# Self-attention over 32 images on one core: another order of work for the first image

## The reference

```python
x = inputs.reshape(B, H * W, c)             # B=32, H*W=1024 tokens, c=256
q = x @ Wq + bq; k = x @ Wk + bk; v = x @ Wv + bv
scores = einsum('bnc,bmc->bnm', q, k) * c ** -0.5
out = (softmax(scores) @ v) @ Wo + bo
# what is returned, _gn being a group norm over 32 groups of 8 channels:
x + attention(_gn(x))
```

## Time and profile before

| | us |
|---|---|
| median of 3 runs (lowest, highest) | 1845.19 (1845.04, 1846.48) |
| the profiled execution | 1844.48 |
| its span, first to last instruction | 1842.8 |
| TensorE busy in the span | 1815.6 (99%) |
| VectorE busy | 1663.2 (90%) |
| ScalarE busy | 984.1 (53%) |
| mean granted clock of TensorE | 0.994 |

### The profile page before, as it was taken

The page is one execution under the profiler, slowest core; times in us unless marked ns, Lnnn a source line. Parts: engine busy times, 40 slices in busy tenths (PEclk is TensorE's granted clock), DMA queues, the critical chain, the costliest instruction groups (busy, mean ns, idle before and its releaser), DMA issues.

```text
span 1842.8 us, 32692 instructions
## 1 busy us (share of the span) xinstructions
PE 1815.6 (99%) x11562; PEld 1654.1 (90%) x11562; DVE 1663.2 (90%) x2921; ACT 984.1 (53%) x1347; POOL 92.1 (5%) x107
## 2 busy tenths in 40 slices
PE   8899999999999999999999999999999999999997
PEld 7799998999998998989999989989989999899896
DVE  5999999999999999999999999999999999999985
ACT  3645545646546556456455465465564554654652
POOL 0000000000000000000000000000000000000000
PEclk9999999999999999999999999999999999999998
DMA  3111222212222212222122222022221122220211
GB/s 114 58 51 29 68 57 68 68 26 54 68 57 68 62 18 68 57 68 68 36 44 68 57 68 67 12 68 62 63 68 43 37 68 57 68 68 17 62 24 24
DMA packets 29296, 101.92 MB, mean 55 GB/s; under 512 B 3681, under 2 KB 4706, under 8 KB 29282
## 3 DMA queue, kind: packets, MB, share of 16 engines
q0 software_dynamic: 9216, 33.56, 11.7%
q1 hardware_dynamic: 20066, 68.17, 11.2%
HBM read 68.16 MB, written 67.11 MB: 73 GB/s over the span
## 4 chain that ended last, share of the span: by engine, by line
PE 98%; DVE 1%; ACT 0%; DMA 0%; issue 0%; SPq 0%; POOLq 0%
PE ps_s L619 48%; PE ps_o L693 13%; PE ps_o L695 13%; PE ps_o L694 13%; PE ps_o L619 10%; DMA s_buf<-in_L_conv_bq_dram 0%; ACT p_hi L312 0%; ACT s_buf L318 0%; DVE s_buf L485 0%; DVE p_lo L493 0%; PE ps_o L631 0%; DVE s_buf L510 0%; DVE query_max L472 0%; SPq L217 0%; POOLq L66 0%
## 5 line engine op out<-in xcount | busy, mean ns | idle before, releaser
L693 PE MATMUL ps_o<-v_hi,p_hi 128*128 128x258 f32 x2048 | 580.6, 283 | 2.8 <-DVE p_lo L493 2.8
L695 PE MATMUL ps_o<-v_hi,p_lo 128*128 128x258 f32 x2048 | 581.1, 284 | 0.0
L694 PE MATMUL ps_o<-v_lo,p_hi 128*128 128x256 f32 x2048 | 578.4, 282 | 0.0
L312 ACT ACTIVATE p_hi<-s_buf 128x1024 fp32r<-128x1024 f32 x256 | 272.0, 1063 | 527.5 <-DVE s_buf L485 527.5
L619 PE MATMUL ps_s<-g_hi,h_hi 128*128 128x512 f32 x1024 | 399.7, 390 | 7.8 <-ACT s_buf L304 7.7
L619 PE MATMUL ps_s<-g_hi,h_lo 128*128 128x512 f32 x1024 | 400.4, 391 | 0.0
L619 PE MATMUL ps_s<-g_lo,h_hi 128*128 128x512 f32 x1024 | 399.8, 390 | 0.0
L693 PEld LDWEIGHTS ps_o<-v_hi,p_hi 128*128 128x128 f32 x2048 | 389.2, 190 | 5.7 <-issue 2.2
L694 PEld LDWEIGHTS ps_o<-v_lo,p_hi 128*128 128x128 f32 x2048 | 388.9, 190 | 3.0
L695 PEld LDWEIGHTS ps_o<-v_hi,p_lo 128*128 128x128 f32 x2048 | 388.7, 190 | 0.0
L304 ACT ACTIVATE s_buf<-ps_s 128x512 f32<-128x512 f32 x512 | 292.9, 606 | 170.2 <-PE ps_s L619 166.3
(11 more groups left out here) (84 smaller groups left out, 2199.5 us busy)
## 6 DMA issues: line engine op xcount, KB each, us to landing
x_t<-in_x_turned_dram SPq DMA_DIRECT2D x64, 512.0 KB, 3.9
out_dram<-in_x_dram SPq DMA_DIRECT2D x64, 512.0 KB, 7.3
out_dram<-o_buf POOLq DMA_DIRECT2D x64, 512.0 KB, 5.6
s_buf<-in_L_conv_Wq_dram SPq DMA_DIRECT2D x1, 256.0 KB, 3.0
s_buf<-in_L_conv_Wk_dram SPq DMA_DIRECT2D x1, 256.0 KB, 3.0
s_buf<-in_L_conv_Wv_dram SPq DMA_DIRECT2D x1, 256.0 KB
s_buf<-in_L_conv_Wo_dram SPq DMA_DIRECT2D x1, 256.0 KB
s_buf<-in_L_conv_bq_dram SPq DMA_DIRECT2D x1, 1.0 KB, 3.1
```

Of the source, the lines that this page charges most:

```text
L312: nc.scalar.activation(p_hi[c][:, rows, :], s_buf[c][:, rows, :], ACT.Exp, scale=SCALE).then_inc(p_hi_done, 1)
L693: nc.tensor.matmul(ps[:, 0:VC], p_hi[c][:, m, cols], v_hi[:, m, :], start=m == 0, stop=False)
L694: nc.tensor.matmul(ps[:, 0:C], p_hi[c][:, m, cols], v_lo[:, m, :], start=False, stop=False)
L695: last = nc.tensor.matmul(ps[:, 0:VC], p_lo[c][:, m, cols], v_hi[:, m, :], start=False, stop=m == T - 1)
```

## The change

It touches the first image and what stands before it; the loop's body and the last image are the same. SP issues x_t first, then the four weights, then the short vectors. ScalarE copies the turned weights. h of the first image is made in halves of 512 tokens, and `project_g(0)` begins with the first half; TensorE turns Wv before the fold of A. The fold of Wv Wo goes behind the scores of half 0 (into bank `ps_o[2]`), and `project_v(0)` waits for it. VectorE takes image 1's statistics and group norm beside the maxima of half 0, and the row maxima before the rests of v. ScalarE puts `scores_out` of half 1 between the exponentials of half 0.

```diff
             load_turned(0)
             load_weight(0, wq, wqk_in)
             load_weight(1, wk, wqk_in)
-            with nc.allow_non_contiguous_dma(reason="a short vector, once"):
-                sp.dma_start(bq_col, bq.rearrange("(k p) -> p k", p=P)).then_inc(wqk_in, 16)
-            load_turned(0)
             load_weight(2, wv, wvo_in)
             load_weight(3, wo, wvo_in)
...
+                sp.dma_start(bq_col, bq.rearrange("(k p) -> p k", p=P)).then_inc(bq_in, 16)
+                sp.dma_start(bv_col, bv.rearrange("(k p) -> p k", p=P)).then_inc(bias_in, 16)
+            sp.dma_start(bo_row, bo.rearrange("(a n) -> a n", a=1)).then_inc(bias_in, 16)
 # ScalarE
+            turned_out(0)
+            turned_out(1)
+            turned_out(2)
+            first_h_part(0, 0, first_h, first_h_hi)
+            first_h_part(1, 0, first_h, first_h_hi)
+            fold_first(a_hi, ps_a, 1)
+            first_h_part(0, 1, h_done, h_hi_done)
+            first_h_part(1, 1, h_done, h_hi_done)
             act.wait_ge(fold_done, 2)
             for i in range(4):
                 g_part(0, i)
...
+            def first_softmax():
+                fold_first(vo_hi, ps_vo, 3)
+                for i in range(4):
+                    v_part(0, i)
+                exponentials_hi(0, 0, 0)
+                scores_out(0, 1, 0)
+                exponentials(0, 0, 0)
+                scores_out(0, 1, 1)
+                exponentials_hi(0, 0, 1)
+                scores_out(0, 1, 2)
+                exponentials(0, 0, 1)
+                scores_out(0, 1, 3)
+                for i in (2, 3):
+                    exponentials_hi(0, 0, i)
+                    exponentials(0, 0, i)
+                for m in range(4, T):
+                    scores_out(0, 1, m)
 # VectorE
+            turn_back(0)
+            dve.wait_ge(norm_done, 1)
+            first_normalise(0, 0, first_h)
+            first_normalise(1, 0, first_h)
+            first_normalise(0, 1, h_done)
+            first_normalise(1, 1, h_done)
+            first_h_rest(0, 0, first_h_hi, first_h_lo)
+            first_h_rest(1, 0, first_h_hi, first_h_lo)
+            fold_rest(0, a_hi, a_lo, ps_a)
+            first_h_rest(0, 1, h_hi_done, h_lo_done)
+            first_h_rest(1, 1, h_hi_done, h_lo_done)
+            dve.wait_ge(fold_ps, 2)
+            nc.vector.tensor_copy(g_bias[:], ps_gb[:, 0:K]).then_inc(fold_done, 1)
...
+            def second_stats():
+                channel_stats(1)
+                dve.wait_ge(bn_done, 8)
+                channel_sums(1)
+                group_means(1)
+                group_spread(1)
+                maxima(0, 0, 0)
+                group_variance(1)
+                maxima(0, 0, 1)
+                turn_back(1)
+                maxima(0, 0, 2)
+                normalise(1)
+                maxima(0, 0, 3)
+                maxima(0, 0, 4)
+            def first_softmax():
+                part_maxima(0, 0)
+                query_maxima(0, 0)
+                row_maxima(0, 0)
+                fold_rest(1, vo_hi, vo_lo, ps_vo)
+                dve.wait_ge(fold_ps, 4)
+                nc.vector.tensor_copy(out_bias[:], ps_ob[:, 0:C]).then_inc(fold_done, 1)
+                difference(0, 0, 0)
+                for i in range(4):
+                    v_rest(0, i)
+                difference(0, 0, 1)
+                p_rest(0, 0, 0)
+                difference(0, 0, 2)
+                p_rest(0, 0, 1)
+                difference(0, 0, 3)
+                p_rest(0, 0, 2)
+                p_rest(0, 0, 3)
 # TensorE
-            pe.wait_ge(wqk_in, 16 * 3)
+            pe.wait_ge(wqk_in, 16 * 2)
             pe.wait_ge(const_step, 7)
             turn_weight(0)
             turn_weight(1)
+            pe.wait_ge(wvo_in, 16 * 2)
+            turn_weight(2)
             pe.wait_ge(w_turned, 2)
             fold(ps_a, wq_t, wk_t)
+            pe.wait_ge(bq_in, 16)
...
             pe.wait_ge(fold_done, 2)
-            project_g(0)
+            project_g(0, True)
+            def second_fold():
+                fold(ps_vo, wv_t, wo_sb)
+                pe.wait_ge(bv_ready, K)
+                product(ps_ob[:, 0:C], [(bv_wide[:, j, :], wo_sb[:, j, :]) for j in range(K)]
+                        + [(ones[0:1, :], bo_row)], fold_ps)
+                pe.wait_ge(fold_done, 3)
...
                 for m in range(T):
                     scores(b, 0, m)
-                if not first:
+                if first:
+                    second_fold()
+                else:
                     for j in range(TQ):
                         attend(b - 1, 1, j)
                 project_v(b)
```

More of the change, by code:

```diff
@@ L140, in attention_kernel @@
         wqk_in = sem("wqk_in")
+        bq_in = sem("bq_in")
+        bias_in = sem("bias_in")
         wvo_in = sem("wvo_in")
@@ L158, in attention_kernel @@
         norm_done = sem("norm_done")
+        first_h = sem("first_h")
+        first_h_hi = sem("first_h_hi")
+        first_h_lo = sem("first_h_lo")
         h_done = sem("h_done")
@@ L283, in h_parts @@
             def h_parts(b):
-                after(act, s_ps, b * 16)
+                act.wait_ge(s_ps, b * 16)
                 for k in range(K):
@@ L287, in h_parts, with first_h_part @@
                     nc.scalar.activation(h_hi[:, k, :], x_t[:, k, :], ACT.Copy).then_inc(h_hi_done, 1)
+            def first_h_part(k, c, ready, done):
+                act.wait_ge(ready, k + 1)
+                cols = slice(c * Q, (c + 1) * Q)
+                nc.scalar.activation(h_hi[:, k, cols], x_t[:, k, cols], ACT.Copy).then_inc(done, 1)
             def g_part(b, i):
@@ L354, in body @@
                 if first:
[L355 to L361, removed]
+                    first_softmax()
+                else:
+                    softmax_beside(b, 0, lambda i: v_part(b, i))
+                    scores_out(b, 1, 0)
+                    last_exponentials(b, 0)
+                    for m in range(1, T):
+                        scores_out(b, 1, m)
                 if not last:
@@ L424, in normalise, with first_normalise, first_h_rest @@
                                             ALU.subtract, ALU.mult).then_inc(h_done, 1)
+            def first_normalise(k, c, done):
+                cols = slice(c * Q, (c + 1) * Q)
+                nc.vector.tensor_scalar(x_t[:, k, cols], x_t[:, k, cols], norm[:, 0, k:k + 1], norm[:, 1, k:k + 1],
+                                        ALU.subtract, ALU.mult).then_inc(done, 1)
+            def first_h_rest(k, c, ready, done):
+                cols = slice(c * Q, (c + 1) * Q)
+                dve.wait_ge(ready, k + 1)
+                nc.vector.tensor_tensor(h_lo[:, k, cols], x_t[:, k, cols], h_hi[:, k, cols].bitcast(F32),
+                                        ALU.subtract).then_inc(done, 1)
             def h_rest(b, k):
@@ L524, in _ @@
             channel_sums(0)
-            fold_rest(0, a_hi, a_lo, ps_a)
-            dve.wait_ge(fold_ps, 2)
-            nc.vector.tensor_copy(g_bias[:], ps_gb[:, 0:K]).then_inc(fold_done, 1)
             group_means(0)
@@ L534, in _ @@
+            first_h_rest(0, 1, h_hi_done, h_lo_done)
[3 more added lines that the diff above has]
+            for i in range(4):
+                g_rest(0, i)
+            dve.wait_ge(bias_in, 16 * 2)
             for j in range(K):
                 nc.vector.tensor_scalar(bv_wide[:, j, :], ones[:], bv_col[:, j:j + 1], None, ALU.mult).then_inc(bv_ready, 1)
-            turn_back(0)
@@ L575, in next_stats @@
                     dve.wait_ge(bn_done, b * 4 + 8)
-                for step in range(5):
-                    maxima(b, 0, step)
                 if first:
[L581 to L586, removed]
+                    second_stats()
+                    first_softmax()
+                else:
+                    for step in range(5):
+                        maxima(b, 0, step)
+                if last:
                     softmax_beside(b, 0, lambda j: finish(b - 1, 1, j), nothing, lambda i: v_rest(b, i),
                                    nothing, nothing)
-                else:
+                elif not first:
                     softmax_beside(b, 0, lambda j: finish(b - 1, 1, j), nothing, lambda i: v_rest(b, i),
                                    next_stats, lambda: channel_sums(b + 1))
-                if not last:
+                if not first and not last:
                     group_means(b + 1)
@@ L640, in fold, with project_g @@
                             fold_ps if k == K - 1 else None)
-            def project_g(b):
-                pe.wait_ge(h_hi_done, b * 2 + 2)
-                pe.wait_ge(h_lo_done, b * 2 + 2)
+            def project_g(b, first=False):
+                if first:
+                    pe.wait_ge(first_h_hi, 2)
+                    pe.wait_ge(first_h_lo, 2)
+                else:
+                    pe.wait_ge(h_hi_done, b * 2 + 2)
+                    pe.wait_ge(h_lo_done, b * 2 + 2)
                 for i in range(4):
```

(5 more changed lines are left out.)

35 lines of the change are left out of this document (10 added, 25 removed).

## The result

| | before | after |
|---|---|---|
| median of 20 runs, us | 1845.67 | 1842.81 |
| lowest and highest | 1843.68, 1848.46 | 1840.52, 1844.74 |
| profiled execution, its span | 1844.48, 1842.8 | 1843.11, 1841.4 |

The ratio is 0.9985, with a 95% interval of 0.9978 to 0.9991: 2.8 us less (1.7 to 4.1). I had forecast 0.5 less, "no change that can be measured". That was too cautious: the interval leaves out zero, so 20 runs do tell this difference from none, small as it is.

The account below looks back on a forecast made before the run. TensorE, gapless in the loop, was taken as the bound, so only the start of `project_g(1)` could move: -3.5 + 1.2 + 7.9 - 8.3 + 2.2 = -0.5 us, from 1845.19 to 1844.7, range 1841.3 to 1848.0.

Parts of the forecast that it names:

- G1: Start of `project_g(1)`, the first work of image 1; at 75.30 us before the change, forecast near 75.
- Step 4: From the start of `project_g(0)` to that of `project_v(0)`: 24.7 us instead of 16.75, plus 7.9, of which 4.9 new idleness.
- V: Start of `project_v(0)`, at 37.47 us before; forecast 24.7 us after the start of `project_g(0)`.
- Step 5: From `project_v(0)` to `project_g(1)`: 29.5 us instead of 37.8, minus 8.3; old 7.65 stall gone, about 1 us behind VectorE.
- Step 6: Clock at `project_v(0)`: falls in the 4.9 us of idleness, loss 2.2 us, bounds 1.3 and 3.0.
- Step 3: Clock at the start: rises about 13.3, `project_g(0)` at 17.2, gain 3.5; falling afterwards, at half a chance, loses 1.2.
- step 2: From the weights' landing to `project_g(0)`: sum 18.1 us; weights bound the start, halves of h buy nothing.
- Step 1: The loads: bq no longer in front, about 0.7 us; Wk lands at 8.5 us, bounds 7.8 and 9.2.
- The clock holds: Rival: clock rises early in the fold, stays before `project_g(0)`, falls late or never at `project_v(0)`; about 1841.0; chance 0.12.
- The clock falls twice: Rival: no rise in the fold, `project_g(0)` slow for 2.5, `project_v(0)` for 3.0; +2.5 us, 1847.7; chance 0.14.
- The weights are later than reckoned: Rival on the loads: no gain by moving bq away and Wo last; +1.6 us, 1846.3; chance 0.12.
- The stall isn't moved but gone: Rival: VectorE reaches row maxima earlier, idleness before `project_v(0)` under 2 us, clock stays; 1839.5; chance 0.06.

Follow-up runs that it names:

- vo_early: Changed kernel with VectorE's rest of Wv Wo ahead of the chain to the row maxima instead of behind it; ratio to before 0.9954.
- warm_v: Changed kernel with 18 unread matmuls of 512 columns in TensorE's idle stretch before `project_v(0)`; ratio to before 0.9974.
- warm_start: Changed kernel with 22 unread float32 matmuls on TensorE while it waits for Wq and Wk; ratio to before 0.9988.
- old_act: Changed kernel with ScalarE's old order in the softmax of half 0, without the interleaved evictions; ratio to before 0.9999.
- bias_first: Changed kernel with VectorE's copy of the bias of g ahead of the second half's two `h_lo` pieces; ratio to before 0.9973.
- both: Changed kernel with the edits of vo_early and bias_first together; ratio to before 0.9942, median 1834.4 us.
- whole_h: Changed kernel with the first image's h made in pieces of 1024 tokens, all ahead of the rest of A on VectorE; ratio to before 0.9980.
- h_early: Kernel both, with image 1's `h_lo` on VectorE right behind the maxima of half 1 of image 0; ratio to before 0.9945.
- w_first: Changed kernel with Wq and Wk loaded ahead of x_t again, Wv turned after the fold of A and bias products; ratio to before 1.0010.

## Why the prediction was right, and what it mis-sized

**Rows and steps that held.** All of it happens before G1: span less G1 is 1767.5 before and 1766.6 after, 1767.5 and 1767.7 in their repetitions (1844.3 - 76.80, 1840.6 - 72.87). The odd one, 1766.6, goes with a shorter slow stretch of the clock near 1820 us, in the last image (3.4 us, against 6.8 in the other three). *Step 4*: V at G + 24.7 plus the clock's 1.2 was said; 42.94 - 17.27 = 25.7 was measured, with the wait of 4.3 (said 4.9) ended by `vo_lo`. `vo_early` showed that its place alone makes it. Inside this agreement two small errors offset each other: without the slow clock it is 24.2, and the slow clock costs 1.5. *Step 5*: attended tiles with no stall, `project_g(1)` behind VectorE by 1 (1.36 measured), and 29.5 from V to G1 at full clock (29.7 measured). *Step 6*: 2.2 said, 2.2 by `warm_v` against the change's first profile, 1.4 against its second. *Step 3*: the clock fell at or just after G in four profiles (the change twice, `warm_v`, `warm_start`) and not in `vo_early`, `old_act`, `bias_first`, `both`, `whole_h` and `h_early`; the first two of these have the change's own code up to there. It goes either way, near the half chance I gave it. *The halves of h* bought nothing, as step 2 said.

**What was off: the start, and where the sum was hung.** The forecast of G1 was 74.8, and the first profile has 74.84. That hit is luck: this profile happened to have Wk at 8.85 and the clock's rise at 13.7, near the 8.5 and 13.3 that I had assumed, and both are the latest of all. Over eight further profiles with this order of loads Wk was there at 7.43, 7.46, 7.54, 7.67, 7.78, 7.80, 8.09 and 8.42; my lower bound of 7.8 was too high too. The rise came between 10.5 and 13.7. So G is usually 16.0 to 16.5, below the lower bound of 16.6 that step 3 gave to its 17.2.

Step 2's reason was wrong as well. It said that h's norm is done long before the fold and that the weights bound the start, without adding up VectorE's own work from the landing of x_t. That chain (counted from the start of the statistics' last three instructions: statistics, the wait of 1.22 for GpSimd's power, normalising, `h_lo`, `a_lo`, `h_lo`, the bias) takes 10.5 us to G: in the change's second profile, in `warm_start`, and in `w_first`, where the weights are there at 4.5 and G is 4 us later all the same. Only when the fold ends late does VectorE wait in it for `a_hi`: 0.89 us in the change's first profile, 0.30 in `warm_v`. The halves stand in this chain too, but whole pieces take as long in it (`whole_h`, 10.45).

Step 1's 0.7 us for bq isn't borne out either. `w_first` has the same dip in the first loads without bq among them: 136 and 139 GB/s in the microseconds from 4 to 6. Its second piece of x_t, the end of the same 1.5 MB, is waited for until 9.59, no earlier than the 9.22 and 9.05 of the two profiles of before. What bq in front did delay is TensorE, whose wait for the weights included it: its first record is at 5.00 and 5.59 before, 4.53 in `w_first`. Why x_t and then the weights land sooner than the weights and then x_t stays open.

The rest is the base: the profiled execution of before was 1.2 below its median, with G1 1.5 earlier than in its repetition. Mean G1 of two profiles each is 76.05 and 73.86: 2.2 less, between the 2.0 (0.9989) and 2.8 (0.9985) of the timings. By the same means, the start brought 4.7 instead of 3.5 (half of this difference is before's late G in its repetition), G to V cost 8.9 instead of 9.1, and V to G1 brought 6.5 instead of 6.1.

**The rivals.** *The clock holds* didn't happen: in all seven profiles with the wait of 4.3 and no fillers in it, the clock fell within it. *The clock falls twice* is what both profiles of the change have (3.3 or 3.4 us, then 4.9 or 3.0), but this rival also had no rise of the clock in the fold, and the clock rose there each time. *The weights are later than reckoned*: they were earlier in eight of nine profiles. *The stall isn't moved but gone* was ruled out for this order rightly, and is what vo_early is: it had been priced at 1839.5, and the order that reaches it measured 1836.75.

**What stays open.** Which of the clock's courses an execution gets. In the same kernel it rose at 13.7 or 10.7 and was slow for 4.9 or 3.0 us at V, so the code alone doesn't decide it, and two profiles of each don't give how often. Parts of the change were not run by themselves: ScalarE's copies of the turned weights, and image 1's group norm beside the maxima of half 0.

## What to carry to other kernels

When a stall is taken away by moving work, look on the engine's own queue for what the moved work now stands behind: here 0.65 us of VectorE behind 4.1 of maxima cost TensorE 4.3 us and the clock another 1.4 to 2.7. Before saying which load bounds a start, add up the other engine's chain from its own load: here VectorE's 10.5 us from x_t, and not the weights, set it in most profiles. Price an idle stretch of TensorE that ends in a slow clock at its length and half of the slow stretch after it (3.3 us slow cost 1.5, 4.9 cost 2.2). Before hanging a sum of a few microseconds on one profile, set its time beside the spread of the runs; where loads and the clock vary by 1 to 2 us, the range must have that in it from the start.

## What the runs showed of the hardware

The granted clock reads 1.00 from the start of a span until its first change, though TensorE then runs at 1.2 GHz: the fold's records of 256 columns took 657 ns there and 432 after it. Reads of the same 1.5 MB in the same order landed between 7.43 and 8.85 us from one profile to another, a spread of half this change's gain. Matmuls that nobody reads kept the clock up in `warm_v`: with 18 of them over a wait of 4.3 us the granted clock stayed at 1.00, G1 - V was 29.7 instead of 31.9 or 31.1, and VectorE's work beside them was no slower (V at G + 25.8 against 25.7). Idle stretches of 1.94, 1.95, 2.10 and 2.77 us before G were followed by a fall of the clock, others of 1.96, 2.50 and 2.71 weren't: in this range the length of the idle stretch didn't tell the two apart.
